# A four-layer graph network: one-hots and gathered adjacency through DRAM, and a fourth of one product on POOL

## The reference, cut to what matters

```
x = x + L0(h, adj)   # 4 heads: softmax over the neighbours of leaky_relu(p_i + c_j), times h @ weight
x = x + L1(h, adj)   # adj.T @ h, divided by the column sums
x = x + L2(h, adj)   # out = h @ W0.T + T1 @ W1.T + T2 @ W2.T; T1 = adj @ h, T2 = 2 adj @ T1 - h
XW = h @ W;  den = exp(leaky_relu(s_row[:, None] + s_col[None, :], 0.01))      # layer 3
num = adj @ den
att = where(num != 0, den / num, 0)
x = x + adj @ (att @ XW)
```

## Time and profile before

| | us |
|---|---|
| median of 3 runs | 692.52 |
| lowest and highest run | 686.78, 692.58 |
| profiled execution | 690.29 |
| its span, first to last instruction | 688.5 |
| busy: PE, PEld | 569.2, 519.8 |
| busy: DVE | 497.5 |
| busy: ACT | 250.0 |
| busy: POOL | 89.0 |
| mean granted TensorE clock | 0.916 of full speed |

### The profile page before, as it was taken

The page is one execution under the profiler, slowest core; times in us unless marked ns, Lnnn a source line. Parts: engine busy times, 40 slices in busy tenths (PEclk is TensorE's granted clock), DMA queues, the critical chain, the costliest instruction groups (busy, mean ns, idle before and its releaser), DMA issues.

```text
span 688.5 us, 15070 instructions
## 1 busy us (share of the span) xinstructions
PE 569.2 (83%) x5741; PEld 519.8 (76%) x5741; DVE 497.5 (72%) x1001; ACT 250.0 (36%) x401; POOL 89.0 (13%) x81
## 2 busy tenths in 40 slices
PE   1688589999902998598897499999999899999797
PEld 1577589999901565497884299999899899998697
DVE  2853498888385355446767399999999999999611
ACT  2699011121003133365544123433333333333363
POOL 1119000000010001243432000000000000002041
PEclk9995699999755999699998699999999999999999
DMA  8693111111000000000000000000000000000001
GB/s 299 262 371 144 38 48 48 34 44 46 0 1 0 1 1 0 0 1 1 1 1 2 3 1 2 2 1 0 0 0 0 0 0 0 0 1 1 0 17 46
DMA packets 8355, 24.37 MB, mean 35 GB/s; under 512 B 688, under 2 KB 3696, under 8 KB 6256
## 3 DMA queue, kind: packets, MB, share of 16 engines
q1 hardware_dynamic: 7328, 23.10, 9.3%
q10 hardware_dynamic: 976, 0.59, 0.3%
HBM read 22.61 MB, written 1.08 MB: 34 GB/s over the span
## 4 chain that ended last, share of the span: by engine, by line
PE 43%; DVE 17%; issue 6%; ACT 4%; POOL 1%; DVEq 0%; ACTq 0%; POOLq 0%
PE bank L1224 15%; PE bank L1081 10%; PE bank L1059 7%; PE bank L1231 4%; PE bank L1242 4%; DVE h L1345 2%; DVE denw L1736 2%; DVE dTc L1761 2%; DVE tc L1754 2%; ACT yc L843 2%; DVE yc L1768 1%; ACT yc L845 1%; PE bank L1111 1%; DVE stats L1299 1%; DVE e L1643 1%
## 5 line engine op out<-in xcount | busy, mean ns | idle before, releaser
L1224 PE MATMUL bank<-ATc,denc 128*128 128x128 f32 x1024 | 122.5, 278 | 19.5 <-DVE denw L1736 18.6
L1224 PEld LDWEIGHTS bank<-ATc,denc 128*128 128x128 f32 x1024 | 118.1, 194 | 21.9 <-issue 18.9
L1081 PE MATMUL bank<-pcs,Ar 128*128 128x256 f32 x768 | 95.1, 287 | 7.2 <-DVEq L1331 3.7
L1081 PEld LDWEIGHTS bank<-pcs,Ar 128*128 128x128 f32 x768 | 93.9, 196 | 8.8 <-DVEq L1331 4.7
L843 ACT ACTIVATE yc<-bank 128x512 f32<-128x512 f32 x64 | 37.7, 589 | 155.5 <-PE bank L1231 155.5
L537 POOL CAST Ar<-AT 128x2048 fp32r<-128x2048 bf16 x24 | 47.4, 1984 | 312.8 <-PE bank L1231 245.1
L1019 PE MATMUL bank<-whp,G 128*128 128x136 bf16 x768 | 63.1, 226 | 8.9 <-DVE G L1523 8.9
L1242 PE MATMUL bank<-XW,yc 128*128 128x128 f32 x512 | 67.0, 285 | 2.6 <-DVE yc L1768 2.6
L1059 PE MATMUL bank<-pcs,A 128*128 128x385 bf16 x256 | 45.4, 339 | 28.7 <-DVEq L1324 28.7
L1242 PEld LDWEIGHTS bank<-XW,yc 128*128 128x128 f32 x512 | 60.8, 195 | 6.7 <-DVE yc L1768 3.0
L1535 DVE SCALAR_TENSOR_TENSOR zc<-rows,wc,ATc 128x128 f32<-128x128 f32 x192 | 51.8, 347 | 18.7 <-ACT wc L685 18.7
(11 more groups left out here) (202 smaller groups left out, 793.6 us busy)
## 6 DMA issues: line engine op xcount, KB each, us to landing
a<-in_adj SPq DMA_DIRECT2D x16, 1024.0 KB, 6.1
rows<-tau SPq DMA_DIRECT2D x16, 256.0 KB, 3.2
out<-X SPq DMA_DIRECT2D x4, 256.0 KB, 2.2
W<-in_L_gnn_W ACTq DMA_DIRECT2D x1, 192.0 KB, 6.5
attB<-in_L_gnn_att_weight ACTq DMA_DIRECT2D x1, 128.0 KB, 4.7
a3B<-in_L_gnn_a ACTq DMA_DIRECT2D x1, 128.0 KB, 8.9
W<-in_L_gnn_weight ACTq DMA_DIRECT2D x1, 64.0 KB, 1.9
W<-in_L_gnn_W ACTq DMA_DIRECT2D x1, 64.0 KB, 6.9
```

The costliest lines, as they stand in the source:

```text
L1081: last = nc.tensor.matmul(bank[t % 2][:, 0:2 * D], Ar[t % 4][:, kt, :], pieces[:, kt, :], start=kt == 0, stop=kt == T - 1)
L1224: nc.tensor.matmul(bank[c][:, P * k:P * k + P], denc[b][:, part, j0:j0 + P], ATc3[b][:, part, :], start=k == 0 and part == 0, stop=False, ...
```

## The change

It has four parts.

1. In layer 0, `one_hot` makes `G` in two instructions, as layer 3 did. SP stores each tile's `G` (512 KB) to a DRAM tensor `kept_G`, and the gathered adjacency `ATc`, which is f32 now, to `kept_A` (192 KB). `G` and `ATc` are overwritten only once their store has landed. The last chunk's `zc` is computed on its 64 slots only; POOL sets the other half to zero at the start (four memsets), and TensorE's first gather waits for them. The mask that `Eb` carried, `lone`, is stored once into `kept_A`, element by element. The first two one-hots stand ahead of VectorE's `choose`.
2. In layer 3, SP loads `G3` and `ATc3` from DRAM: tiles 0 and 1 once the second product is joined, the others as their buffers come free. VectorE's `one_hot3` and `Eb`, ScalarE's `edges3`, and the adjacency matmuls of TensorE's `gather3` are gone.
3. `times_own` of bank 3 is done by POOL; `refine` of that bank waits for it.
4. POOL reaches its casts for the last product after these sixteen products.

```diff
@@ sync: layer 0, after the load of rows for tile it
+                    keep_one_hot(it)
+                    if it > 0:
+                        keep_adjacency(it - 1)
+                keep_adjacency(T - 1)
+                for b in range(2):
+                    sp.wait_ge(g_kept[b], 16 * HT)
+                    sp.wait_ge(a_kept[b], 16 * HT)
+                sp.wait_ge(lone_ready, 1)
+                sp.dma_start(kept_A.rearrange("(t p) c -> t p c", p=P)[:, P - 1, 0:P].rearrange("t i -> i t"), lone[:, :],
+                             allow_slow_non_contiguous=True).then_inc(lone_kept, 16)
+                sp.wait_ge(lone_kept, 16)
+                sp.wait_ge(acc_used, 2 * NG + 2)
+                fetch(0)
+                fetch(1)
+            def keep_one_hot(it):
+                sp.wait_ge(g_ready, 2 * it + 2)
+                sp.dma_start(kept_G[P * it:P * it + P, :], G[it % 2][:, :, :].rearrange("p j s -> p (j s)")
+                             ).then_inc(g_kept[it % 2], 16)
+            def keep_adjacency(it):
+                sp.wait_ge(e_copied, it + 3)
+                sp.dma_start(kept_A[P * it:P * it + P, :], ATc[it % 2][:, :, :].rearrange("p c i -> p (c i)")
+                             ).then_inc(a_kept[it % 2], 16)
+            def fetch(it):
+                b = it % 2
+                if it >= 2:
+                    sp.wait_ge(g3_used, it + 1)
+                sp.dma_start(G3[b][:, :, :].rearrange("p j s -> p (j s)"), kept_G[P * it:P * it + P, :]
+                             ).then_inc(g3_loaded[b], 16)
+                if it >= 2:
+                    sp.wait_ge(num3_bank, 4 * it + 4)
+                sp.dma_start(ATc3[b][:, :, :].rearrange("p c i -> p (c i)"), kept_A[P * it:P * it + P, :]
+                             ).then_inc(a3_loaded[b], 16)
+            def by_slots3():
+                for it in range(2, T):
+                    fetch(it)
@@ gpsimd
             def by_slots():
+                for b in range(4):
+                    nc.gpsimd.memset(zc[b][0:HP, NC - 1, :, :], 0.0).then_inc(zc_zero, 1)
                 pool.sem_inc(diag_ready, 48)
+                pool.wait_ge(zc_zero, 4)
+            def times_own(it, b, c):
+                pool.wait_ge(own3_ready, it + 1)
+                pool.wait_ge(y_ready, 4 * it + c + 1)
+                own = dTc[b][:, 4 * c:4 * c + 4, :].rearrange("p j i -> p (j i)")
+                nc.gpsimd.tensor_tensor(own, own, yc[b][c][:, :], ALU.mult).then_inc(pd_ready, 1)
             def by_slots3():
+                sweep(pool, lambda it, b: times_own(it, b, 3))
                 pool.wait_ge(num3_bank, 4 * (T - 1) + 8)
@@ scalar
                 act.wait_ge(pc_ready, it + 3)
+                if within(it, -2):
+                    act.wait_ge(a_kept[b % 2], 8 * (it - b % 2))
-                if within(it, 2):
-                    edges3(it + 2, b)
@@ tensor
             def by_slots():
                 pe.wait_ge(pieces0_ready, 25)
+                pe.wait_ge(zc_zero, 4)
             def gather3(it, b):
-                pe.wait_ge(g3_ready, 2 * it + 2)
+                pe.wait_ge(g3_loaded[b], 8 * (it - b) + 16)
                 pe.wait_ge(e3_copied, it + 1)
-                pe.wait_ge(at3_ready, it + 1)
                 for c, (first, end) in enumerate(CHUNKS):
                     for jt in range(first, end):
-                        nc.tensor.matmul(bank[4 + b][:, P * c:P * c + P], G3[b][:, jt, :],
-                                         AT[:, jt, bass.ds(it * P, P)], start=jt == first, stop=jt == end - 1 and c > 0)
-                    if c == 0:
-                        nc.tensor.matmul(bank[4 + b][:, 0:P], Eb[:, bass.ds(it, 1), :].rearrange("p o s -> p (o s)"),
-                                         identb[:, :], start=False, stop=True)
...
             def num3(it, b, p):
                 pe.wait_ge(denc_ready, 3 * it + 3)
-                pe.wait_ge(at3_ready, it + 3)
+                pe.wait_ge(a3_loaded[b], 8 * (it - b) + 16)
@@ vector
             def one_hot(it, b):
                 dve.wait_ge(gathered, it + 1)
+                if it >= 2:
+                    dve.wait_ge(g_kept[it % 2], 16 * (it // 2))
+            dve.wait_ge(choice, 1)
+            one_hot(0, 0)
+            one_hot(1, 1)
             choose(dve, 0, *counted(by_slots, over_all))
@@ vector, layer 3
-            one_hot3(0, 0)
-            one_hot3(1, 1)
-            nc.vector.memset(Eb[:, :, :], 0.0).then_inc(rp_ready, 1)
             def refine(it, b, c):
-                dve.wait_ge(yd_ready, n + 1)
+                if c < 3:
+                    dve.wait_ge(yd_ready, 3 * it + c + 1)
+                else:
+                    dve.wait_ge(pd_ready, it + 1)
             def tile3(it, b):
-                if within(it, 2):
-                    one_hot3(it + 2, b)
...
-                    times_own(it, b, c)
+                    if c < 3:
+                        times_own(it, b, c)
```

More of the change, by code:

```diff
@@ L106, in gnn_stack @@
         wc = [at(f"wc_{b}", B + 32 + 1.75 * b, [P, NC, WC]) for b in range(4)]
-        ATc = [at(f"ATc_{b}", B + 39 + 0.75 * b, [P, NC, P], BF16) for b in range(2)]
+        ATc = [at(f"ATc_{b}", B + 39 + 1.5 * b, [P, NC, P]) for b in range(2)]
         rows = [at(f"rows_{b}", B + 44 + 2 * b, [P, H * P]) for b in range(2)]
@@ L195, in gnn_stack @@
         mk = const("mk", [P, T])
+        lone = const("lone", [P, T])
         over3 = const("over3", [P, 1])
@@ L274, in gnn_stack @@
         rows_loaded = [sem(f"rows_loaded{b}") for b in range(2)]
+        g_kept = [sem(f"g_kept{b}") for b in range(2)]
+        a_kept = [sem(f"a_kept{b}") for b in range(2)]
+        lone_ready = sem("lone_ready")
+        lone_kept = sem("lone_kept")
+        zc_zero = sem("zc_zero")
+        g3_loaded = [sem(f"g3_loaded{b}") for b in range(2)]
+        a3_loaded = [sem(f"a3_loaded{b}") for b in range(2)]
         pc_ready = sem("pc_ready")
@@ L557, in over_all3 @@
                 pool.wait_ge(logits_ready, 2)
+                for b in range(2):
+                    pool.wait_ge(g3_loaded[b], 16)
+                    pool.wait_ge(a3_loaded[b], 16)
                 pool.wait_ge(qt_ready, NG)
@@ L703, in by_slots @@
                 copy_output(T - 1)
+                for b in range(2):
+                    act.wait_ge(g_kept[b], 16 * HT)
+                    act.wait_ge(a_kept[b], 16 * HT)
                 act.sem_inc(bc_copied, 48)
@@ L805, in over_all3 @@
             def over_all3():
+                for b in range(2):
+                    act.wait_ge(g3_loaded[b], 16)
+                    act.wait_ge(a3_loaded[b], 16)
                 broadcast_copies(52)
@@ L1195, in gather3 @@
             def gather3(it, b):
-                pe.wait_ge(g3_ready, 2 * it + 2)
+                pe.wait_ge(g3_loaded[b], 8 * (it - b) + 16)
                 pe.wait_ge(e3_copied, it + 1)
-                pe.wait_ge(at3_ready, it + 1)
                 for c, (first, end) in enumerate(CHUNKS):
                     for jt in range(first, end):
-                        nc.tensor.matmul(bank[4 + b][:, P * c:P * c + P], G3[b][:, jt, :],
-                                         AT[:, jt, bass.ds(it * P, P)], start=jt == first, stop=jt == end - 1 and c > 0)
-                    if c == 0:
-                        nc.tensor.matmul(bank[4 + b][:, 0:P], Eb[:, bass.ds(it, 1), :].rearrange("p o s -> p (o s)"),
-                                         identb[:, :], start=False, stop=True)
-                    for jt in range(first, end):
-                        last = nc.tensor.matmul(bank[4 + b][:, P * NC + 6 * c:P * NC + 6 * c + 6], G3[b][:, jt, :],
+                        last = nc.tensor.matmul(bank[4 + b][:, 6 * c:6 * c + 6], G3[b][:, jt, :],
                                                 rp[:, jt, :, :].rearrange("p w k -> p (w k)"),
@@ L1717, in edges3 @@
                 dve.wait_ge(g3_used, it + 3)
-                dve.wait_ge(at3_ready, it + 3)
-                pieces = bank[4 + b][:, NC * P:NC * P + 6 * NC].rearrange("p (c w k) -> p c w k", w=2, k=3)
+                pieces = bank[4 + b][:, 0:6 * NC].rearrange("p (c w k) -> p c w k", w=2, k=3)
                 ul = rc[b][:, :, :].unsqueeze(3)
```

79 lines of the change are left out of this document (35 added, 44 removed).

## The result

The changed kernel takes 660.75 us (median of 4 runs, 658.13 to 667.16), the kernel before 691.75 in the same comparison; the ratio is 0.958, interval 0.9496 to 0.9664. The prediction was 659 us in a range of 650 to 673. The profiled execution took 659.75 us, its span is 657.8, so 30.7 us shorter than the span of before; the sum had forecast 31.6. A run more than 1.5% above the fastest of its kernel is left out of the ratio; one of the two runs of one experiment is such a run, so that experiment has no ratio.

What follows compares the result with a forecast made beforehand. VectorE and TensorE were both taken as nearly full in layer 3's tiles. Terms: -24.8 (13 tiles), -1.8 (tile 14), +1.5 (tail), -6.0 (way in), -0.5 (layer 0) = -31.6; 690.3 to 658.7, so 659 us, range 650 to 673.

Steps and rivals of the forecast that it cites:

- the sum: All stretches of the profiled execution together: 31.6 us less, from 690.3 to 658.7 us.
- TensorE's unbroken row: Layer 3's tiles: TensorE's work without a gap, 13.75 us a tile, making TensorE longer than VectorE by 0.8 us.
- handovers between two full engines: Layer 3's tiles: 0.15 us a tile added for handovers, giving 13.9 us a tile.
- Rival A: Layer 3's tiles: VectorE and POOL hold each other up, VectorE stays the bound; 14.1 to 14.6 a tile, 662 to 668, chance 0.26.
- POOL's multiply: Layer 3, bank 3's `times_own`: 1.15 us on POOL, result not awaited, half its price (0.6 us) lost on VectorE.
- a sign of error: Layer 3: the prediction called itself wrong if POOL's multiply is above 1.5 us.
- The way in: Last `rp` to layer 3's first `num3`: 6.0 us less without ScalarE's adjacency copy, bounds 4 and 7.5.
- what follows runs as before: Tile 0 of layer 3: after its first reciprocal nothing changes, so the tile is worth nothing.
- The tail: Tile 15 to the last product: 1.5 us longer, bounds -2 and +4, as POOL's two casts come after its sixteenth multiply.
- Layer 0's start: Up to layer 0's first gather: gain 0.5 us from one-hots ahead of the choice, bounds 2.4 and -1.
- Rivals B and C: B: late stores make layer 0's steps wait, 675, chance 0.06. C: `lone`'s element-wise store delays layer 3's fetches, 759, chance 0.05.
- the spread case: `lone`'s store of 2,048 pieces, spread over 16 engines at 0.14 us a packet: 18 us.

## Why the prediction was right

**The tile.** The step that carries four fifths of the gain held: I set TensorE's unbroken row at 13.75 us from starts in one tile, and it is 13.83. The timeline of one tile, where TensorE has no gap, shows where the 0.08 lie:

```profile
484.48 3.82 PE L1286 MATMUL bank<-ATc,denc 128*128 128x128 f32 x32
...
497.85 0.55 PE L1271 MATMUL bank<-rp,G 128*128 128x6 bf16 x16
498.32 3.83 PE L1286 MATMUL bank<-ATc,denc 128*128 128x128 f32 x32
```

From `num3` to the gather it is 13.37 us, where I had taken 0.09 off the 13.39 of before as a slow start after idle time: that part stays without any idle time. The 0.15 us that I had put on top for handovers between two full engines don't exist as such, since TensorE never waits; that one error makes up for half of the other is luck. VectorE's idle time, 0.6 us a tile in the changed kernel, is what took up POOL's hold-ups. Rival A is excluded by TensorE's full row, and by the tile with two banks on POOL.

**POOL's multiply** was mis-sized. I had 1.15 us, and called 1.5 a sign of error; it lasts 1.31 to 2.19, 1.76 on average. In the middle tiles short and long ones take turns. POOL's multiply in two neighbouring tiles, and VectorE's `refine` beside each:

```profile
484.85 1.31 POOL L668 TENSOR_TENSOR dTc<-dTc,yc 128x512 f32<-128x512 f32 x1 [11.69 <-ACT yc L923]
498.63 2.17 POOL L668 TENSOR_TENSOR dTc<-dTc,yc 128x512 f32<-128x512 f32 x1 [12.47 <-ACT yc L923]
```

```profile
484.95 1.76 DVE L1824 SCALAR_TENSOR_TENSOR yc<-tc,dTc 128x512 f32<-128x512 f32 x1
...
498.99 0.68 DVE L1824 SCALAR_TENSOR_TENSOR yc<-tc,dTc 128x512 f32<-128x512 f32 x1
```

In the one tile VectorE is held up, in the next POOL is long and `refine` is not. That POOL waits for VectorE there fits the timeline, but was not tried by itself. The error cost nothing, because TensorE is the bound and nobody waits for the product. In the kernel before, where VectorE is the bound, the multiply gained nothing: what VectorE gave up came back as hold-ups.

The rule of the Trainium skill, page "SBUF — State Buffer", section "Who interferes with whom", by which one of the two engines fully blocks for an instruction of the other: the runs agree in these places, `refine` lasting 1.76 us beside a multiply of 1.31, `denw` 1.75 beside another and 2.38 beside a cast. Whether that reaches the time depends on the path: in the changed kernel it does only in the tail.

**The way in** held: 6.49 against 6.0. VectorE's branch shows as 3.24 us where I took 3.5 from layer 0.

**Tile 0** was forecast at no change and lost 1.38 us. The step that failed is "what follows runs as before": the first `num3` ran at half the clock for 6.46 us. A shorter way in left TensorE with less work ahead of it, 4.9 us busy in 7.5 with the clock at 0.50, where before it had 7.4 in 14.0 at 0.62. That this is the cause is not shown, since two profiles with the same way in (two banks on POOL, and the kernel without POOL and with casts on ScalarE) begin tile 0 at the full clock; the third quick one, with the adjacency matmuls kept, has more work on the way in.

**The tail** lost 2.35 against 1.5, by the mechanism forecast: the casts came after POOL's last multiply and held VectorE. The last matmuls of `u3` start 20.57 us into the tail where before it was 18.26. Moving the casts took 2.3 us off; the tail fell by 3.8 in that profile, the rest being TensorE's clock. **The last product** is 1.46 us longer, which I had not counted: its granted clock is 0.94 instead of 1.00. With POOL's multiply undone it takes 37.4 us to the end all the same, where I had expected 35.7, and with POOL's multiply alone 35.6. Without POOL and with the casts on ScalarE one profile has 37.1 and the other 35.6. So POOL's multiply is not its cause; what is, the runs don't settle.

**Layer 0's start** gained 1.7 against 0.5: I gave POOL the branch time seen on VectorE and TensorE. **Rivals B and C**: the stores are all but hidden even when doubled, and `lone` took 14.5 us, near the 18 of the spread case.

My sum came within 1 us by luck, because errors cancel: the first three stretches and the 13 tiles gave 2.8 us more than I had set, tile 0, the tail and the last product 3.7 less.

## What to carry to other kernels

When two engines are both nearly full, price a cut by the other engine's unbroken row, read from starts in the timeline, and look for a cut on both: here one alone was worth nothing in the tiles, the other half of both. Don't count work handed to GpSimd beside a full VectorE as taken off VectorE: here one bank relieved it of nothing where it was the bound (it worked 15.40 us a tile without and 15.45 with POOL's help), a second bank of 0.46 us a tile where TensorE was the bound, and neither shortened a tile. And follow a queue to its end: an instruction put ahead of others on an idle engine moved two casts of 2 us into the one place where they were waited beside.

## What I had not expected of the hardware

- POOL's multiply of 128x512 f32 took from 1.31 to 2.19 us in the same loop, in turns short and long, and held VectorE's operation beside it in the short ones.
- The time at a choice (the wait for the flag, its load to a register, the branch) differs by engine: 0.8 us on POOL from the flag to its next instruction (71.44 to 72.26), 4.5 on TensorE (to 75.94), 3.2 and 3.5 of idle time on VectorE. That nothing else ends TensorE's 4.5 is read from the timeline and was not tried.
- The same stretch runs at another granted clock from profile to profile, though TensorE has the same work before it: the first `num3` takes 3.8 or 6.3 to 6.7 us, the first wide product 29.3 or 30.9, the last one 31.0 to 33.7. Where TensorE is full, the 13 middle tiles run at 1.00 throughout and repeat to 0.01 us a tile in nine profiles of seven kernels, while the runs of the changed kernel spread over 8 us (653.72 to 661.69 in one comparison). Its three runs of 653.7 to 655.2 us have a mean granted clock of 0.914 to 0.922, its three of 660.2 to 661.7 one of 0.903 to 0.905; I take the clock for the reason, and did not test it.
